# Bias network of an attention block: centred weights, ScalarE's squares for the variance, a new order of stages

## What is computed

```python
def ln(x, g, eps=1e-05):
    mean = x.mean(axis=-1, keepdims=True)
    var = ((x - mean) ** 2).mean(axis=-1, keepdims=True)
    return (x - mean) * jax.lax.rsqrt(var + eps) * g

def rel_pos_bias(n, w0, b0, g0, w1, b1, g1, w2, b2, dtype):
    pos = jnp.arange(-n + 1, n, dtype=dtype)[:, None]
    h = jax.nn.silu(ln(pos @ w0 + b0, g0))     # [.., 512]
    h = jax.nn.silu(ln(h @ w1 + b1, g1))       # w1 is [512, 512]
    h = h @ w2 + b2                            # w2 is [512, 16]
    ...
```

## Time and profile before

| | us |
|---|---|
| three runs, median | 1786.67 (1785.74 to 1787.05) |
| the profiled execution | 1786.81 |
| its span | 1784.5 |
| busy: TensorE, VectorE, ScalarE, GpSimd | 1604.5, 1407.2, 1141.8, 1421.9 |
| bias network, VectorE's first to the maximum | 18.12 to 151.54 |

### The profile page before, as it was taken

One profiled execution on the slowest core, in us unless ns is written; L12 is line 12 of the kernel. 1 busy time (PEld: TensorE's weight loads), 2 busy tenths in 40 slices (PEclk: granted clock), 3 DMA queues, 4 the chain that ended last, 5 costly groups with the idle time before them and its releaser, 6 DMA issues.

```text
span 1784.5 us, 46777 instructions
## 1 busy us (share of the span) xinstructions
PE 1604.5 (90%) x15122; PEld 1079.6 (60%) x15122; DVE 1407.2 (79%) x2569; ACT 1141.8 (64%) x2195; POOL 1421.9 (80%) x934
## 2 busy tenths in 40 slices
PE   3786897899999999998995898799999999998997
PEld 1443554577777777776552455477777777776553
DVE  4885898788888888884765798688888888887576
ACT  1342555587787788777441555477887887787441
POOL 3564666799999999997673566799999999999574
PEclk9998999899999999998997999899999999999998
DMA  6000012011112111100023002021111111110023
GB/s 186 1 0 21 25 29 59 13 37 35 28 37 49 25 37 37 29 21 14 30 71 102 25 29 65 1 47 26 38 37 25 37 37 41 26 32 13 7 71 100
DMA packets 41302, 68.84 MB, mean 39 GB/s; under 512 B 8880, under 2 KB 9392, under 8 KB 41136
## 3 DMA queue, kind: packets, MB, share of 16 engines
q1 hardware_dynamic: 36512, 58.12, 13.3%
q10 hardware_dynamic: 4640, 8.54, 1.4%
HBM read 58.11 MB, written 8.54 MB: 37 GB/s over the span
## 4 chain that ended last, share of the span: by engine, by line
PE 44%; issue 26%; POOL 17%; DVE 9%; ACT 1%; DVEq 1%; POOLq 1%; DMA 1%; SPq 0%; ACTq 0%
PE ps L1162 21%; PE ps L1135 10%; PE ps L1138 10%; DVE work L930 5%; POOL rinv L491 4%; POOL work L496 4%; POOL work L523 3%; POOL qo L454 2%; POOL work L541 2%; PE ps L1204 1%; DVE work L958 1%; POOL rstd L486 1%; DVE denom L955 1%; POOL work L498 1%; POOL work L462 1%
## 5 line engine op out<-in xcount | busy, mean ns | idle before, releaser
L511 POOL TENSOR_TENSOR work<-work 128x1024 f16<-128x1024 f32 (+2 forms) x576 | 978.2, 1733 | 44.2 <-ACT work L644 41.6
L930 DVE SCALAR_TENSOR_TENSOR work<-ps,tab 128x1024 f32<-128x1024 f32 (+3 forms) x640 | 668.7, 1059 | 141.3 <-PE ps L1138 139.4
L644 ACT ACTIVATE work<-work 128x1024 f32<-128x1024 f32 (+3 forms) x640 | 578.2, 924 | 207.3 <-DVE work L930 203.4
L1162 PEld LDWEIGHTS ps<-vals,work 128*128 128x128 bf16 (+1 forms) x8704 | 545.3, 98 | 115.8 <-POOL work L511 2.2
L1162 PE MATMUL ps<-vals,work 128*128 128x129 f16 x8704 | 600.5, 221 | 1.9 <-POOL work L511 1.8
L1135 PE MATMUL ps<-qo,kT 128*128 128x512 f16 (+3 forms) x1280 | 344.2, 351 | 20.8 <-DVE work L930 15.0
L1138 PE MATMUL ps<-qo,kT 128*128 128x512 f16 (+3 forms) x1280 | 342.1, 349 | 0.0
L1106 PE MATMUL ps<-wq,work 128*128 128x512 f16 x768 | 178.0, 390 | 20.4 <-DVE work L863 20.4
L1138 PEld LDWEIGHTS ps<-qo,kT 128*128 128x128 f16 x1280 | 123.2, 98 | 117.5 <-issue 3.3
L1204 PE MATMUL ps<-wout,work 128*128 128x512 f16 x768 | 175.0, 385 | 0.0
L1106 PEld LDWEIGHTS ps<-wq,work 128*128 128x128 f16 x768 | 74.6, 100 | 113.5 <-issue 34.2
(11 more groups left out here) (131 smaller groups left out, 1727.0 us busy)
## 6 DMA issues: line engine op xcount, KB each, us to landing
tab<-bias_table SPq DMA_DIRECT2D x64, 512.0 KB, 4.7
work<-in_x SPq DMA_DIRECT2D x32, 256.0 KB, 2.6
tab<-in_x SPq DMA_DIRECT2D x32, 256.0 KB, 2.7
out_x<-work ACTq DMA_DIRECT2D x32, 256.0 KB, 2.2
work<-in_L_cond_Wq SPq DMA_DIRECT2D x1, 2048.0 KB, 12.8
work<-in_L_cond_Wout SPq DMA_DIRECT2D x2, 1024.0 KB, 10.3
qo<-in_L_cond_w SPq DMA_DIRECT2D x1, 1024.0 KB, 9.5
qo<-in_L_cond_b SPq DMA_DIRECT2D x2, 256.0 KB, 4.2
```

The source lines that it names most:

```text
L511: pool.tensor_tensor(low[:, k % LRING, :, c0:512], probs[:, r, :, c0:512], high[:, r, :, c0:512], ALU.subtract).then_inc(low_pool, 1)
L644: act.activation(probs[:, k % RING, :, c0:512], probs[:, k % RING, :, c0:512], ACT.Exp).then_inc(expd, 1)
L930: dve.scalar_tensor_tensor(out=probs[:, k % RING, :, c0:512], in0=ps[:, 2 * (k % 2):2 * (k % 2) + 2, c0:512], scalar=SCORE, in1=tab[:, :, ...
L1162: last = pe.matmul(ps[:, sum_bank(i, q), (t % SUMS) * VS:(t % SUMS + 1) * VS], parts[:, rings[part], e, s * P:(s + 1) * P], vals[:, j, :], ...
```

## The change

- The means per row are gone. The mean over the 512 outputs is taken out of `w0`, `b0` and `b1` on VectorE (`centred`) and out of the rows of `w1`: VectorE sums them (`w1_means`), ScalarE adds the negative mean (`ACT.Identity` with a bias). The hidden rows then have mean zero.
- The variance comes from ScalarE: `ACT.Square` over 513 elements with a row sum (`accum_out`); the last of them is a constant that stands for epsilon. bn_stats, bn_aggr, the epsilon and L807 are gone. GpSimd multiplies the hidden row by the gain without waiting for the variance, and the power goes into Silu as its scale.
- The stages are issued by `pipeline`, all steps written out, with lags 0 to 4, and in another order on each engine.
- The split of weights is done in four parts of `Wq` (steps 5, 8, 11, 14; 1024 elements) and four of `Wout` (steps 6, 9, 12, 15; two of 512), and likewise the null product and its sums.
- The loads come in another order, and setup work of VectorE, GpSimd and TensorE that stood ahead of the tiles now stands within its steps 0 to 3 (`m_setup`, `null_weigh`, `m_ternary`).

The core of the diff; of VectorE's and TensorE's stages only the new side is shown. Left out: bookkeeping of semaphores and tensors, `ternary_weights`, `small_setup` and `null_key`, which hold the instructions that stood ahead of the network before, and the start values of semaphores.

```diff
+def since(eng, semaphore, count):
+    if count > 0:
+        eng.wait_ge(semaphore, count)
+def pipeline(n, stages):
+    for s in range(n + max(lag for _, lag in stages)):
+        for stage, lag in stages:
+            if 0 <= s - lag < n:
+                stage(s - lag)
...
-        hid = carve(flat, 2, 2, D)
-        hid_n = carve(flat, 2, D)
+        hid_e = carve(flat, 2, 2, D + 1)
+        hid = hid_e[:, :, :, 0:D]
+        hid_q = carve(flat, 2, D // 2 + 1).bitcast(BF16)
...
+        SPLIT_Q = {5 + 3 * c: c for c in range(KC)}
+        SPLIT_O = {6 + 3 * c: c for c in range(KC)}
...
+            for dst, src in ((w0_b, w0[0, :]), (b0_b, b0), (g0_b, g0)):
+                sp.dma_start(dst, bc(src)).then_inc(ld_in, 16)
+            sp.dma_start(w1_sb, w1.rearrange("(c p) n -> p c n", p=P)).then_inc(ld_w1, 16)
+            for dst, src in ((b1_b, b1), (g1_b, g1)):
+                sp.dma_start(dst, bc(src)).then_inc(ld_mid, 16)
             sp.dma_start(packed_sb, packed.rearrange("(p n) -> p n", n=D)).then_inc(ld_tern, 16)
...
+            sp.dma_start(w2_sb, w2.rearrange("(c p) n -> p c n", p=P)).then_inc(ld_w2, 16)
+            for dst, src in ((nb_b[:, :], null_bias), (qs_b[:, :], q_scale), (qk_scale[:, :], k_scale),
                              (nk_b, cond[0, :]), (ws_b[:, :], w_scale)):
...
+                sp.dma_start(dst, bc(src)).then_inc(ld_small, 16)
+            sp.dma_start(b2_c[:, :], b2.rearrange("(p o) -> p o", o=1)).then_inc(ld_small, 16)
+            sp.dma_start(nb_c[:, :], null_bias.rearrange("(p o) -> p o", o=1)).then_inc(ld_small, 16)
...
             def m_gain(layer):
-                def f(t, u):
-                    s = M[layer]
-                    pool.wait_ge(s["n"], t + 1 + 2)
-                    pool.wait_ge(s["s"], t + 1)
-                    pool.tensor_tensor(hid_g[:, layer, u, :], hid_n[:, layer, :], (g0_b, g1_b)[layer],
+                def f(t):
+                    s, u = M[layer], t % 2
+                    if layer == 0:
+                        since(pool, ld_in, 16 * 3)
+                    else:
+                        since(pool, ld_mid, 16 * 2)
+                    pool.wait_ge(s["h"], t + 1)
+                    since(pool, s["s"], t - 1)
+                    pool.tensor_tensor(hid_g[:, layer, u, :], hid[:, layer, u, :], (g0_b, g1_b)[layer],
                                        ALU.mult).then_inc(s["g"], 1)
                 return f
-            def null_weigh(t, u):
+            def m_power(layer):
+                def f(t):
+                    s, u = M[layer], t % 2
+                    pool.wait_ge(s["q"], t + 1)
+                    since(pool, s["s"], t - 1)
+                    pool.tensor_tensor(m_rstd[:, layer, u, :], m_var[:, layer, u, :], minus_half[:, 0:1], ALU.pow
+                                       ).then_inc(s["rstd"], 1)
+                return f
+            def null_weigh(t):
+                if t == 2:
+                    pool.wait_ge(null_done, 1)
+                    pool.tensor_tensor(nk_r[:, :], nk_sm[:, :], minus_half[:, 0:1], ALU.pow).then_inc(null_rs, 1)
+                if t not in SPLIT_Q:
+                    return
+                c = SPLIT_Q[t]
                 pool.wait_ge(ld_proj, 16 * 3)
                 pool.wait_ge(setup_chain, 5)
-            pool.wait_ge(ld_mlp, 16 * 12)
-            skewed(pool, NT, [(m_power(0), 0), (m_gain(0), 1), (m_power(1), 5), (m_gain(1), 6), (null_weigh, 7)])
+                since(pool, wn_sum, c)
+                pool.tensor_tensor(null_prod.rearrange("p (h d) -> p h d", d=DH),
+                                   wq_in[:, c * H * DH:(c + 1) * H * DH].rearrange("p (h d) -> p h d", d=DH),
+                                   nk_n.unsqueeze(1).to_broadcast([P, H, DH]), ALU.mult).then_inc(wn_prod, 1)
+            pipeline(NT, [(m_gain(0), 0), (null_weigh, 0), (m_power(0), 0), (m_gain(1), 2), (m_power(1), 2)])
...
+            act.wait_ge(w_sums, 2)
+            for c in range(KC):
+                act.activation(w1_sb[:, c, :], w1_sb[:, c, :], ACT.Identity, bias=w_mean[:, c:c + 1]
+                               ).then_inc(w_centred, 1)
+            def m_square(layer):
+                def f(t):
+                    s, u = M[layer], t % 2
+                    act.wait_ge(s["h"], t + 1)
+                    since(act, s["rstd"], t - 1)
+                    since(act, s["q"], t)
+                    act.activation(hid_q[:, layer, 0:D + 1], hid_e[:, layer, u, :], ACT.Square, scale=D ** -0.5,
+                                   accum_out=m_var[:, layer, u, :]).then_inc(s["q"], 1)
+                return f
             def m_silu(layer):
-                def f(t, u):
-                    s = M[layer]
-                    act.wait_ge(s["g"], t + 1 + 1)
+                def f(t):
+                    s, u = M[layer], t % 2
+                    act.wait_ge(s["g"], t + 1)
+                    act.wait_ge(s["rstd"], t + 1)
+                    since(act, s["T"], t - 1)
+                    act.activation(hid_s[:, layer, u, :], hid_g[:, layer, u, :], ACT.Silu,
+                                   scale=m_rstd[:, layer, u, :]).then_inc(s["s"], 1)
+                return f
+            def m_copy(layer):
+                def f(t):
+                    s, u = M[layer], t % 2
                     act.wait_ge(s["T"], t + 1)
-                    act.activation(hid_s[:, layer, u, :], hid_g[:, layer, u, :], ACT.Silu).then_inc(s["s"], 1)
-                return f
-            def m_copy(layer):
-                def f(t, u):
-                    s = M[layer]
-                    act.wait_ge(s["T"], t + 1 + 2)
-                    act.wait_ge(s["mm"], t + 1)
+                    since(act, s["mm"], t - 1)
                     act.copy(hidT[:, layer, u, :, :], ps[:, layer, :].rearrange("p (c r) -> p c r", c=KC)
                              ).then_inc(s["Tc"], 1)
                 return f
-            def w_high(t, u):
-                                   scale=WSCALE).then_inc(wo_high, 1)
+            def w_high(t):
+                if t in SPLIT_Q:
+                    c = SPLIT_Q[t]
+                    act.wait_ge(w_gain, 1)
+                    act.wait_ge(ld_proj, 16 * 3)
+                    act.activation(wq[:, 0, c, :], wq_in[:, c * H * DH:(c + 1) * H * DH], ACT.Copy,
+                                   scale=gn_w[:, c:c + 1]).then_inc(wq_high, 1)
+                if t in SPLIT_O:
+                    c = SPLIT_O[t]
+                    act.wait_ge(ld_out, 16 * 4)
+                    for n in range(2):
+                        act.activation(wout[:, 0, n * KC + c, :], wout_in[n][:, c * D:(c + 1) * D], ACT.Copy,
+                                       scale=WSCALE).then_inc(wo_high, 1)
...
-            act.wait_ge(w_gain, 1)
-            skewed(act, NT, [(m_copy(0), 3), (m_copy(1), 8), (m_silu(0), 2), (m_silu(1), 7), (w_high, 6)])
+            pipeline(NT, [(m_silu(1), 3), (m_silu(0), 1), (m_square(0), 0), (m_square(1), 2), (m_copy(1), 3),
+                          (m_copy(0), 1), (w_high, 0)])
...
+            def centred(vector, k):
+                dve.tensor_reduce(v_mean[:, k:k + 1], vector, AX.X, ALU.add).then_inc(centre, 1)
+                dve.wait_ge(centre, 3 * k + 1)
+                dve.tensor_scalar(v_mean[:, k:k + 1], v_mean[:, k:k + 1], -1.0 / D, None, ALU.mult).then_inc(centre, 1)
+                dve.wait_ge(centre, 3 * k + 2)
+                dve.tensor_scalar(vector, vector, v_mean[:, k:k + 1], None, ALU.add).then_inc(centre, 1)
+            dve.wait_ge(ld_in, 16 * 3)
+            centred(w0_b, 0)
+            centred(b0_b, 1)
+            dve.wait_ge(centre, 6)
+            dve.wait_ge(consts, 13)
+            def w1_means():
+                dve.wait_ge(ld_w1, 16)
+                dve.tensor_reduce(w_mean[:, :], w1_sb, AX.X, ALU.add).then_inc(w_sums, 1)
+                dve.wait_ge(w_sums, 1)
+                dve.tensor_scalar(w_mean[:, :], w_mean[:, :], -1.0 / D, None, ALU.mult).then_inc(w_sums, 1)
...
+            def w_low(t):
+                if t in SPLIT_Q:
+                    c = SPLIT_Q[t]
+                    dve.wait_ge(w_gain, 1)
+                    dve.wait_ge(ld_proj, 16 * 3)
+                    dve.wait_ge(wq_high, c + 1)
+                    dve.scalar_tensor_tensor(out=wq[:, 1, c, :], in0=wq_in[:, c * H * DH:(c + 1) * H * DH],
+                                             scalar=gn_w[:, c:c + 1], in1=wq[:, 0, c, :],
+                                             op0=ALU.mult, op1=ALU.subtract).then_inc(wq_low, 1)
+                if t in SPLIT_O:
+                    c = SPLIT_O[t]
+                    dve.wait_ge(ld_out, 16 * 4)
+                    dve.wait_ge(wo_high, 2 * c + 2)
+                    for n in range(2):
+                        dve.scalar_tensor_tensor(out=wout[:, 1, n * KC + c, :], in0=wout_in[n][:, c * D:(c + 1) * D],
+                                                 scalar=WSCALE, in1=wout[:, 0, n * KC + c, :],
```

(48 more changed lines are left out.)

213 lines of the change are left out of this document (57 added, 156 removed).

## The result

The changed kernel takes 1767.4 us (1765.72 to 1768.19), the kernel before 1786.2 beside it (1785.58 to 1787.05): a ratio of 0.9898 [0.9887, 0.991], 18.8 us less. 1776.4 was forecast, 10.4 less than the profiled execution before; the time lies 2.1 under the stated range, which began at 1769.5. The profiled execution took 1767.12 (span 1765.3).

A forecast was written before the change was run, and what follows sets the result against it. VectorE was taken as the bound. 29.3 + 96.6 (14 x 6.9) + 2.8 + 1.7 = 130.4, with 10.7 behind it 141.1 instead of 151.54; 1786.8 - 10.4 = 1776.4 us, range 1769.5 to 1787.

The forecast's parts named there:

- Statistics and the loop: Each step of the bias network: VectorE loses about 3 us and stops being the bound; steps take 6.9 us.
- the chain named: In a step: eight matmuls, addition of `b1`, square, previous tile's copy and second product, then next matmuls: 6.87 us.
- Head: Before the steps: first(0), tile 0's product with `w1`, at 22.2 us instead of 31.21; first(1), tile 1's, at 29.3.
- Weights in four parts: In the steps with a part of `Wq`, VectorE's work ends 0.7 us late, four times: 2.8; `Wout` parts 0.
- Clock: On TensorE in the steps: one group of eight matmuls takes 5.40 us instead of 3.70, 1.7; bounds 0 and 6.8.
- Tail: From first(15), the last tile's product with `w1`, to the reduction over the bias row: 10.7 us, ending at 141.1.
- What follows it is unchanged: Everything behind the bias row's reduction stays the same, so its start 10.4 us earlier gives 1776.4.
- all small terms at their lower bounds: Case, chance 0.04: read-out (2.1), weight parts (2.8), clock (1.7) and second table load (1.3) at lower bounds, 1768.5 us.

The follow-up runs named there:

- `copy_first`: The changed kernel with ScalarE's two copies of a step issued ahead of the square of layer 1, nothing else changed: 1756.52 us, 0.9839 of the kernel before.
- `reordered`: The changed kernel with both squares behind the copies, GpSimd's layer 1 instructions ahead of layer 0's power, VectorE's weight parts one step later: 1752.79 us, 0.9823.
- `sums_twice`: The changed kernel with each null row sum done twice, 1.21 us more on VectorE at each part of `Wq`: 1776.26 us, 0.9946 of the kernel before.
- `sums_busy`: The changed kernel with each null row sum done twice and five unused bf16 products in TensorE's wait from the fifth step on: 1772.69 us, 0.9933.

## Why the prediction was wrong, step by step

- Statistics and the loop: right. 6.9 a step was forecast, 6.80 measured, by the chain named, with TensorE idle for 1.24 where 1.2 was forecast. `copy_first` and `reordered` show it to be this chain. The sum is better than its terms: from the group to the addition it is 3.84 (3.74 forecast), square and read-out together cost 0.63 until the copy starts (0.79 forecast; the read-out is busy 0.19, but adds about 0.09). 14 steps of 0.1 make 1.4 too much.
- Head: right. first(0) 22.2 against 22.00, first(1) 29.3 against 29.83 (30.57 in the second profile), two table loads of 1.28 as forecast. The drain that the Trainium skill ("ScalarE: Activation LUTs", section "What ACT_TABLE_LOAD costs") adds to each switch of tables is not to be seen: the load of 12.79 ends at 14.07 and the centring starts at 14.08.
- **Weights in four parts: the first step that failed.** 0.7 late at each part of `Wq`, 2.8 in all, was forecast; 0.03 was measured (6.82 against 6.79). The difference started at 7.42 of the step, as forecast (7.45). But the forecast laid VectorE's instructions end to end; in the trace each starts 0.07 to 0.09 before the one ahead of it ends (72.44 + 1.21 = 73.65, next 73.56; 73.82 + 0.73 = 74.55, next 74.48), so mostly for that reason the hidden row ends at 10.74 of the step and not at 11.05: 0.3 of the 0.7. Another 0.16 is the square with its read-out, 0.63 where 0.79 was laid, and the rest is in the forecast itself, whose own terms give about 0.55 and not 0.7. The hidden row's square then ends as square1 becomes ready: 74.59 and 75.22 stand back to back, with no room. `sums_twice` shows how near it was: 1.21 more on VectorE gave 1.15 a step, so 0.06 was left. That the parts cost nothing hangs on these 0.06 us and is in part luck. The term was mis-sized by 2.7, though its place and mechanism were right.
- **Clock: the second.** One slow group, 1.7, was carried over from a stage in which TensorE idled over 2 us; none came, in a step that idles 1.24. `sums_twice` and `sums_busy` show that such groups come with waits of 2.4 (three of four) and go when part of the wait is filled.
- Tail: 10.7 forecast, 11.21 measured, 9.92 in the second profile. The forecast took its turn (0.85) and second product (1.3) between the two levels of the clock, and the two profiles have one level each.
- These sum to 141.1 - 136.27 = 4.8: 1.4 + 2.7 + 1.7 of steps, less 0.5 for first(1) and 0.5 for the tail.
- **What follows it is unchanged: the third, and the one that took the time out of the range.** Its instructions are unchanged, but its time was 3.9 shorter in the profile, 1.0 to 3.9 by the pairs of profiles. With 4.8 + 3.9 = 8.7 the difference of the profiled execution from the forecast (1776.4 - 1767.1 = 9.3, the remaining 0.6 being in the main time around the span, 1.8 instead of 2.3) is accounted for. The 4.8 of the stage alone would have given 1771.6, inside the range.
- The range: all small terms at their lower bounds were a case of 0.04, at 1768.5, which the range from 1769.5 left out. The two largest of them, parts and clock, came out near zero together, and the range held nothing for the rest of the span, which alone differs by up to 4.5 us between profiles.

Open: why the clock stays down longer at some places of the rest in one execution than in another, and whether the moment at which the stage ends has a part in it (the two profiles of after differ by 2.0 in the rest, those of before by 0.9); what makes the differences at the first two of the three places; the old tail, which was read and not tried; and what of the head's other 3.1 belongs to which of the edits in it.

## What to carry to other kernels

When a bound engine is unloaded, the next bound can be an order and not an engine: here the steps gained nothing until an instruction of another tile was moved from ahead of the copy that TensorE waits for, and then 11 us came from that one line. Count head and tail by themselves; all that this change gained in its stage lay there, and two thirds of the head's gain was the order of the loads. And compare the untouched rest of the span in two profiles of one kernel before a few us are put down to an edit.
